# An audio tower on one core: the attention stage's loop of two-batch turns written out as straight-line code

## The reference

```
h = tokenizer(x)                 # importance by a 3-layer gelu net, cumulative sum,
                                 # pooling weights Wt, 750 -> 375 tokens per batch
h = h + attn(layernorm(h))       # 8 heads of 64; q, k, v through a 1x1 and a 3-tap
                                 # depthwise causal convolution; ALiBi bias, causal mask
h = h + moe(layernorm(h))        # 16 experts, each takes its top 375 of 6000 tokens,
                                 # plus a shared two-layer network
```

```
xn  = layernorm(h)
q, k, v = taps(wq1 @ xn, wqd), taps(wk1 @ xn, wkd), taps(wv1 @ xn, wvd)
sim = q @ k.T * scale - slope[head] * |i - j|     # masked where j > i
out = softmax(sim) @ v @ wout.T
```

## Time and profile before

| | |
|---|---|
| median of 3 runs | 1566.63 us |
| the profiled execution | 1568.55 us, of which the span is 1566.8 us |
| PE busy | 1354.8 us (86%) |
| PEld busy | 1089.1 us (70%) |
| DVE busy | 952.7 us (61%) |
| ACT busy | 671.4 us (43%) |
| POOL busy | 264.4 us (17%) |
| instruction fetches by DMA | queue 8: 29 packets, 0.48 MB; queue 14: 54 packets, 0.44 MB |
| mean granted TensorE clock | 0.924 of full speed |

### The profile page before, as it was taken

How to read it: one execution, slowest core, us unless ns; L and a number is a source line. 1 busy time by engine, 2 the same in 40 slices (tenths; PEclk the granted TensorE clock), 3 DMA queues, 4 the chain that set the end, 5 groups by cost and what they waited for, 6 DMA issues and landing times. The chain is left out here.

```text
span 1566.8 us, 26688 instructions
## 1 busy us (share of the span) xinstructions
PE 1354.8 (86%) x7905; PEld 1089.1 (70%) x7905; DVE 952.7 (61%) x3107; ACT 671.4 (43%) x1759; POOL 264.4 (17%) x262
## 2 busy tenths in 40 slices
PE   6999999999369999989999899999997896466663
PEld 5999999999356777766767667677665685355553
DVE  3433434334569898879878798788874566621211
ACT  2334334333235655656546565456653341021211
POOL 6000000000010001001110000100000400178885
PEclk9999999999679999999999999999998898687877
DMA  4000000000100000000000000000000112044542
GB/s 106 17 15 20 20 10 20 20 10 20 35 11 10 2 22 23 22 21 17 10 17 21 21 20 10 14 21 12 12 12 20 28 34 60 6 79 81 97 82 39
DMA packets 93851, 43.86 MB, mean 28 GB/s; under 512 B 31295, under 2 KB 90088, under 8 KB 93752
## 3 DMA queue, kind: packets, MB, share of 16 engines
q1 hardware_dynamic: 69960, 36.25, 8.5%
q0 software_dynamic: 23808, 6.69, 3.3%
HBM read 29.52 MB, written 10.18 MB: 25 GB/s over the span
## 5 line engine op out<-in xcount | busy, mean ns | idle before, releaser
L783 ACT ACTIVATE P<-P,nmax 125x375 f32<-125x375 f32 (+2 forms) x384 | 189.1, 494 | 292.1 <-DVE nmax L923 291.9
L287 PE MATMUL bank<-h1hl,W2hl 128*128 128x376 f32 x1536 | 278.0, 336 | 2.9 <-DVE h1hl L402 2.9
L287 PEld LDWEIGHTS bank<-h1hl,W2hl 128*128 128x128 f32 x1536 | 264.0, 189 | 3.1 <-DVE h1hl L402 3.1
L624 PE MATMUL bank<-QK 64*125 64x375 f32 (+2 forms) x768 | 197.8, 391 | 13.4 <-DVE nmax L923 13.4
L624 PEld LDWEIGHTS bank<-QK 64*125 64x125 f32 x768 | 112.8, 185 | 75.8 <-DVE nmax L923 25.0
L364 ACT ACTIVATE h<-bank,b2c 128x375 f32<-128x375 f32 x128 | 73.5, 574 | 207.3 <-PE bank L287 207.3
L923 DVE CUSTOM_DVE_ANT_0 P<-bank,nbias 125x375 f32<-125x375 f32 (+2 forms) x384 | 139.7, 413 | 2.6 <-PE bank L624 2.5
L1569 ACT ACTIVATE hE<-bank,EB 128x375 f32<-128x375 f32 x64 | 36.7, 573 | 199.0 <-PE bank L1544 196.4
L680 PE MATMUL bank<-WVT,xnThl 128*125 128x512 f32 x432 | 115.7, 413 | 3.0 <-DVE QK L972 3.0
L913 DVE TENSOR_SCALAR P<-P,prec 125x375 f32<-125x375 f32 (+2 forms) x384 | 111.9, 347 | 4.5
L865 POOL TENSOR_SCALAR lnve<-lnmv 125x3 f32<-125x3 f32 x32 | 10.1, 315 | 575.6 <-DVE lnmv L891 575.6
(11 more groups left out here) (196 smaller groups left out, 2363.4 us busy)
## 6 DMA issues: line engine op xcount, KB each, us to landing
X<-in_x_dram SPq DMA_DIRECT2D x34, 375.0 KB
EW<-in_L_ffn_w_dram SPq DMA_DIRECT2D x32, 256.0 KB
token_table<-row SPq DMA_DIRECT2D x16, 210.9 KB
tTall<-tT SPq DMA_DIRECT2D x16, 187.5 KB, 2.3
out_dram<-oS SPq DMA_DIRECT2D x16, 187.5 KB
tTall<-in_L_tok_W_dram SPq DMA_DIRECT2D x1, 1024.0 KB, 7.1
EB<-in_L_ffn_b_dram SPq DMA_DIRECT2D x16, 62.5 KB
tok<-token_table,ids POOLq DMA_INDIRECT x48
```

The lines of the kernel that those rows point to most:

```text
L287: last = nc.tensor.matmul(bank[4 + m % 2][:, :NE], W2hl[:, a, k, m * 128:(m + 1) * 128], h1hl[:, p, b, k], start=(k == 0 and n == 0), stop ...
L624: last = nc.tensor.matmul(bS[unit][:PT_, at:at + w], QK[r:r + DH, 0, c, i * PT_:(i + 1) * PT_], QK[r:r + DH, 1, c, :w], start=True, stop=True)
L783: nc.scalar.activation(P[:, h % 4, SEG[q]:SEG[q] + w], P[:, h % 4, SEG[q]:SEG[q] + w], ACT.Exp, bias=nmax[:, h % 4, q:q + 1], scale=-1.0, ...
```

## The change

The loop is gone. All 21 bodies are written out, and `b` is a Python number in all of them. The constants LOOP0 and LOOP1 go with it.

```diff
             FIRST, LAST = -3, B + 1
-            LOOP0, LOOP1 = 3, 13
...
             def bodies(eng, body):
 
-                for b in range(FIRST, LOOP0):
+                for b in range(FIRST, LAST + 1):
                     body(b, b % 2)
-                with eng.Fori(LOOP0, LOOP1 - 1, 2) as i:
-                    body(i, LOOP0 % 2)
-                    body(i + 1, (LOOP0 + 1) % 2)
-                for b in range(LOOP1, LAST + 1):
-                    body(b, b % 2)
```

## The result

The median fell from 1566.65 us to 1526.74 us (1526.17 to 1527.32, 4 runs), a ratio of 0.9744 with a 95% interval of 0.9727 to 0.9761. The forecast was 1528.9 us in a range of 1523 to 1539 us. Run once more beside the last experiments, the same kernel gave 1527.63 us (1526.37 to 1530.16, 5 runs). The profiled execution took 1526.38 us, its span 1524.6 us.

A forecast was written before the change was run, and what follows sets the result against it. PE was taken to bound block two's written-out bodies, with the loop adding DVE fetch stalls and register arithmetic. Removing returns (21.7 us) and arithmetic (16.0 us) gains 37.7 us: 1566.63 to 1528.9 us, range 1523 to 1539 us.

The forecast's parts named there:

- (a): Block two's four loop returns, where DVE waits for instruction fetches: removing them gains 21.7 us, 5.4 us each.
- (b): Register arithmetic in block two's looped bodies, mainly on DVE: removing it gains 16.0 us, 1.6 us per body.
- the releaser in slots 3 to 5: In block two's looped bodies DVE releases PE's scores there and sets the pace; in straight code PE's own issue does.
- (c): Eight more bodies of code to fetch on all five engines: cost inside (b); alone, 0 to 5.4 us per late fetch.
- late-code rival: Straight code reaches DVE late, 5.4 us per fetch; one in each of ten bodies gives 1583 us; chance beyond break-even 0.04.
- clock rival: PE's clock falls in each straight body, costing 10 us over ten: 1538.9 us; chance 0.15 shared with returns alone.
- rival of the returns alone: Only block two's returns matter, bodies stay near 45.9 us: 1544.9 us; chance 0.15 shared with the clock.

The follow-up runs named there:

- the last experiments: Block four's two loops written out: with block two's loop on all engines but DVE, 1522.33 us; in the otherwise unchanged written-out kernel, 1522.76 us.
- the nine-body pass: Against the kernel before, bodies 3 to 11 became one single loop pass, waits and addresses still from registers, and body 12 was written out: 1540.03 us.

## Why the prediction was right

(a) and (b) together: 37.7 us forecast, 37.8 us measured in the ten bodies. The body to compare with was well chosen: 44.33 us in body 2, and 44.30 to 44.34 us in all ten afterwards.

The split between them was off. I took the loop bodies away from the returns as the price of the arithmetic (16.0 us). One pass without returns gives 45.67 - 44.33 = 1.34 us a body, so 13.4 us for the arithmetic and 24.4 us, or 6.1 us each, for the returns, against 21.7 and 5.4. The 24.4 us hold the falls of the clock behind the returns too and, by about 1.0 us, the fall in body 12 that follows no return. The error cancels in the sum, since I had split a total that is the difference of two rows, ten looped bodies and ten times body 2; that the sum came out so well says nothing for the split. The total leans on the choice of body 2 and not on knowing the causes. The 0.34 us at some fetches remain argued only, and so does how the 1.34 us divide among register instructions, spare increments, addresses and longer code.

That DVE is the engine that matters, on both counts, was inferred from one kind of wait and from the releaser in slots 3 to 5. The pair of kernels with the loop on DVE alone and on all but DVE shows it outright. One inference on the way was too strong: queue 14 isn't DVE's alone. About 7 of its 25 fetches in the ten written-out bodies are for other engines, so the five in bodies 1 and 2 needn't all have been DVE's. In the loop the reading stands, 31 fetches with every engine looped and 38 with DVE alone looped, seven more for the others.

(c) The new code cost nothing, as assumed. Queue 8 has 46 fetches in the whole kernel in place of 29, 17 more where some 20 were expected. The late-code rival had no case: not one wait of DVE for issue in ten bodies. The clock rival had none there either, 1.00 throughout; it showed itself in bodies 14 and 15, outside the change, and went in favour of the first measurement. The two medians, 1526.74 and 1527.63 us, lie 2.2 and 1.3 us below the forecast's 1528.9. Falls of this size could make that difference, but executions without a profile don't show where they gained.

The rival of the returns alone is refuted by the nine-body pass at 1540.03 us: without returns, 13 us above the written-out kernel.

## What to carry to other kernels

Compare a loop body with the same body written out before or after the loop; where the two differ, the row is the forecast. Look for an engine with an "issue" wait at the return, and write out that engine's code first, or make its pass short enough; here it alone carried the whole loss. Whether registers cost anything has to be tried engine by engine. In this loop those of DVE (41 of 46 us busy) cost 1.34 us a body and those of PE nothing, though PE is the bound; yet 64 register operations on PE cost 3.5 us in block four's short loops, where PE is the engine on the path.

## What the runs showed of the hardware that I had not expected

- A short loop over code that is held isn't free on DVE: four passes of one increment, one register operation and one branch stopped it for 1.24 us. How much of that is the return wasn't taken apart.
- Fetches missed by PE and DVE at one return cost no more than DVE's miss alone (4.9 us, or 5.6 us by the medians, against 5.4 to 6.1 us), though DVE's own wait grew from 3.85 to 4.86 us.
- With DVE written out, the ten bodies were quicker when the four other engines looped: 442.37 and 442.34 us in two such kernels, 443.23 and 443.25 us in two profiles of the one with no loop. Which of the four it is wasn't tried, and with DVE in the loop it is the other way round (481.05 us with all in it, 480.66 us with DVE alone).
- The same idle gap of PE in body 14, 0.64 us in both profiles compared, was followed by a fall of the clock in one execution and not in the other, while the gaps at the four returns, 1.46 to 1.79 us, were followed by one each time in the kernel before.

```profile
1128.26 0.97 PE L624 MATMUL bank<-QK 64*125 64x375 f32 x3 [0.64 <-DVE nmax L923]
```
```profile
1089.69 0.97 PE L618 MATMUL bank<-QK 64*125 64x375 f32 x3 [0.64 <-DVE nmax L917]
```

The first row is of the kernel before (half clock from 1130.87 us on for 3.42 us), the second of the written-out kernel's first profile (1.00).
